# Second attention of a two-layer gated block: the unread matrix product behind each step is kept in the first of eight rounds only

## The reference, cut to what matters

```
x = x + tanh(g_xattn[0]) * attention0(layernorm(x), ctx)
x = x + tanh(g_ffn[0])   * quantised_ffn(layernorm(x))
query = (layernorm(x) @ w_q.T + b_q)   # 8 x 100 x 256, 16 heads
key, value = ctx @ w_k.T + b_k, ctx @ w_v.T + b_v   # 8 x 361 x 256
attn = softmax(query @ key^T / 4)      # per head, 100 x 361
x = x + tanh(g_xattn[1]) * ((attn @ value) @ w_o.T + b_o)
x = x + tanh(g_ffn[1])   * top2_of_8_experts(layernorm(x))
```

## Time and profile before

| | |
|---|---|
| median of 3 runs | 711.89 us (711.44 to 716.47) |
| the profiled execution | 715.0 us, span 713.3 us |
| mean granted TensorE clock in it | 0.867 of full |
| PE / DVE / ACT / POOL busy over the span | 75% / 60% / 42% / 21% |
| unread products, L1628 | 142 recorded, 49.2 us of PE busy time |
| second attention, rounds 0 to 7 | 398.4 to 511.2 us of the span |

### The profile page before, as it was taken

How to read it: one execution, slowest core, us unless ns; L and a number is a source line. 1 busy time by engine, 2 the same in 40 slices (tenths; PEclk the granted TensorE clock), 3 DMA queues, 4 the chain that set the end, 5 groups by cost and what they waited for, 6 DMA issues and landing times. The chain is left out here.

```text
span 713.3 us, 16026 instructions
## 1 busy us (share of the span) xinstructions
PE 533.2 (75%) x5585; PEld 381.5 (53%) x5585; DVE 430.0 (60%) x898; ACT 298.3 (42%) x480; POOL 146.4 (21%) x184
## 2 busy tenths in 40 slices
PE   0372778889878988736448898998754299999994
PEld 0261345556555656523223465666534288888884
DVE  7724567566666775466752777876467674444441
ACT  1074224555555445403304476775534132332221
POOL 1200002111111111100036212012122213434322
PEclk9995758999999986868859699998965599999998
DMA  8030673444534630000073578995293002122110
GB/s 254 6 108 21 106 150 83 111 108 105 120 96 107 162 91 24 1 0 1 0 144 90 168 142 163 207 159 111 62 346 107 29 17 39 29 40 43 31 26 1
DMA packets 73249, 64.34 MB, mean 90 GB/s; under 512 B 33326, under 2 KB 65750, under 8 KB 73190
## 3 DMA queue, kind: packets, MB, share of 16 engines
q1 hardware_dynamic: 61816, 41.78, 26.3%
q0 software_dynamic: 8224, 21.06, 11.0%
q10 hardware_dynamic: 3152, 0.71, 0.5%
HBM read 48.59 MB, written 15.92 MB: 90 GB/s over the span
## 5 line engine op out<-in xcount | busy, mean ns | idle before, releaser
L458 PEld LDWEIGHTS PS<-QS,KS 112*120 112x120 f16 (+2 forms) x896 | 81.9, 143 | 36.1 <-ACT PT L521 14.5
L458 PE MATMUL PS<-QS,KS 112*120 112x100 f16 (+2 forms) x896 | 92.5, 229 | 11.3 <-ACT PT L521 9.8
L569 DVE CUSTOM_DVE_ANT_0 PS<-PS,maskv 100x461 f32<-100x461 f32 x128 | 80.5, 646 | 14.4 <-PE PS L427 13.1
L572 DVE TENSOR_REDUCE mx<-PS 100x1 f32<-100x361 f32 x128 | 63.6, 529 | 36.2 <-PE PS L430 35.1
L521 ACT ACTIVATE PT<-PS,ctxb 120x400 f32<-120x400 f32 (+1 forms) x96 | 56.8, 593 | 51.9 <-PE PS L458 50.8
L521 ACT ACTIVATE PT<-PS 120x400 f32<-120x400 f32 (+1 forms) x128 | 63.1, 502 | 35.8 <-PE PS L458 33.3
L1969 PE MATMUL PS<-aT,WE 128*128 128x128 f16 x960 | 75.0, 221 | 0.3 <-issue 0.2
L1969 PEld LDWEIGHTS PS<-aT,WE 128*128 x960 | 66.2, 98 | 7.8 <-issue 1.4
L427 PE MATMUL PS<-KS,QS 65*100 65x461 f16 x128 | 51.4, 406 | 15.4 <-DVE mx L569 14.9
L779 POOL TENSOR_SCALAR_AFFINE_SELECT PT<-PT 100x400 f32<-100x400 f32 x32 | 17.6, 551 | 193.0 <-ACT PT L521 193.0
L1984 PE MATMUL PS<-WE,hidden_high 128*128 x320 | 55.6, 272 | 1.4 <-DVE hidden_low L2145 1.4
(11 more groups left out here) (301 smaller groups left out, 1072.5 us busy)
## 6 DMA issues: line engine op xcount, KB each, us to landing
share<-in_L_ffn_w_dram POOLq DMA_DIRECT2D x13, 1024.0 KB, 7.0
k_scratch<-share SPq DMA_DIRECT2D x32, 180.5 KB, 2.7
KS<-k_scratch SPq DMA_DIRECT2D x32, 180.5 KB, 3.7
KS<-k_scratch SPq DMA_DIRECT2D x64, 90.2 KB, 5.8
QS<-q_scratch SPq DMA_DIRECT2D x64, 50.0 KB, 2.5
v_scratch<-xn SPq DMA_DIRECT2D x8, 385.7 KB
values_staged<-v_scratch SPq DMA_DIRECT2D x8, 385.7 KB
WE<-in_L_ffn_w_dram POOLq DMA_DIRECT2D x2, 1024.0 KB, 8.6
```

The lines of the kernel that those rows point to most:

```text
L458: last = nc.tensor.matmul(bank[0:kn, i * T:(i + 1) * T], KS[p][:, h, k0:k0 + kn], QS[p][:, h, :], start=True, stop=True)
L569: nc.vector.tensor_tensor_reduce(rows, rows, maskv[:, :], 1.0, -BIG, ALU.add, ALU.max, mx[p][:, h:h + 1]).then_inc(s_smf, 1)
L572: nc.vector.tensor_reduce(mx[p][:, h:h + 1], sm_bank[h % 2][0:T, 0:TC], X, ALU.max).then_inc(s_smf, 1)
```

## The change

The unread product behind a step is issued only in round 0. In rounds 1 to 7 TensorE goes from the transposed scores of the step straight to what follows. That takes 84 of the 96 products inside the rounds away. The 46 in front of the rounds stay. No wait, no semaphore count and no other instruction is touched.

```diff
                         pe_ST(pe, j, o, t, 1, STN, 2 * B)
-                        unread()
+                        if first:
+                            unread()
                         if not first:
                             if t == PVL1:
```

## The result

| | before | after |
|---|---|---|
| median (lowest to highest) | 714.13 us (711.44 to 716.47) | 731.77 us (727.48 to 735.16) |
| executions | 4 | 4 |
| the profiled execution | 715.0 us, span 713.3 | 734.6 us, span 732.9 |
| mean granted TensorE clock in it | 0.867 | 0.793 |
| rounds 1 to 7 at a granted clock of 1.00 | all but some 7 us | 4 us |

The change makes the kernel slower by 17.6 us. The ratio is 1.0245 (1.0162 to 1.0328). The forecast was 716, with a range up to 720.5; it was worked out on a median before of 711.89 us, of the three executions known then.

A forecast was written before the change was run, and what follows sets the result against it. TensorE seemed the bound, with VectorE and DMA close behind. Changes of -0.2, +1.95, +1.95 and -0.9 us (transfer-limited savings, clock losses) gave +2.8; between 714.7 and 717.8 it took 716 us, range 708 to 720.5.

The forecast's parts named there:

- The upper bound of the gain: Rounds 1 to 7: removing 84 unread products of 0.22 us each frees at most 18.5 us of TensorE's work.
- VectorE's floor: Full-clock round with no transfer in the way: VectorE's 10.7 us plus 1.4 us of hand-overs, 12.1 us.
- The transfer's floor: Rounds 2, 4 and 6 start only when queries land behind the 1 MB load, 13.55 to 14.63 us after its issue.
- I expect the clock to fall at each of these three starts: Starts of rounds 2, 4 and 6: longer waits for queries and thinner work drop TensorE to half clock.
- I take 11 us: Half-clock stretch assumed in each of rounds 2, 4 and 6, costing 2.4 us apiece (bounds 1.5 and 3.3).
- The half-clock round, 15.4 us: A whole round without unread products at half clock, bound by TensorE: 15.4 us against 12.1 at full clock.
- An odd round that is still at half clock costs little more: Odd rounds: the next start waits for the transfer anyway, so half clock there adds little.
- C: Rival: the clock falls and stays down for whole rounds, each even round costing 3.3 us; +6.1, so 720 us; chance 0.21.
- D: Rival: queries issued earlier land earlier, so rounds 1 to 7 go by VectorE; 702 us; chance 0.05.

The follow-up runs named there:

- half_and_light: Kernel before with 256-column unread products in rounds 1 to 7 and, from the fourth on, expert-weight loads cut to a quarter (output not the reference's): ratio 0.9912.
- half_cols: Kernel before with unread products of rounds 1 to 7 cut from 512 to 256 columns: ratio 1.0017, median over all ten executions 721.5 us.
- ballast_even_rounds: Kernel before with the 12 unread products kept in rounds 0, 2, 4 and 6 and none in 1, 3, 5 and 7: ratio 1.0066.
- late_load: Kernel before with GpSimd issuing each load of expert weights six steps later, size unchanged: ratio 0.9999.
- change_light_load: The changed kernel with expert-weight loads cut to a quarter from the fourth on (output not the reference's): ratio to before 1.0244.
- ballast_odd_rounds: Kernel before with unread products kept in rounds 0, 1, 3, 5 and 7 and none in 2, 4 and 6: ratio 1.0013.
- quarter_cols: Kernel before with unread products of rounds 1 to 7 cut from 512 to 128 columns: ratio 1.0230.
- burst_8_at_start: The changed kernel plus 8 unread products behind the scores of step 0 in each of rounds 1 to 7: ratio to before 1.0008.
- alt_steps: Kernel before with 512-column unread products behind even steps only in rounds 1 to 7: ratio 0.9966, median over all ten executions 716.2 us.
- change_short_maxima: The changed kernel with row maxima of the second attention taken over the first 90 of 361 columns: ratio to before 1.0191.
- burst_at_start: The changed kernel plus 16 unread products at step 0 of each of rounds 1 to 7: ratio to before 1.0160.

## Why the prediction was wrong, point by point

*The upper bound of the gain, 84 times 0.22 us: right, and never reached.* The burst shows 3.45 us for 16 unread products, 0.216 each.

*VectorE's floor, 12.1 us: right in kind, 0.4 too low.* The same round at full clock took 12.47 and 12.50 us in the two kernels in which it kept the clock. The bounds, 10.7 and 13.3, held it, and it is not why the forecast failed. half_and_light fits: 1.0 us less work for TensorE made a round 0.37 us shorter.

*The transfer's floor: right in kind.* With less ballast the waits grew at the start of round 2 (1.38 to 1.61 in half_cols) and of round 4 (0.69 to 1.85), and with the small loads all waits were gone. The 2.5 us that were forecast were not seen in them; behind the thin round of ballast_even_rounds it is 1.67. My reasoning was by order as well (the queries queue behind the load); late_load shows that a later issue gains nothing. In the changed kernel, however, this floor of about 14 us is not reached, since its rounds take 17.2.

*"I expect the clock to fall at each of these three starts": this step failed.* It took the earlier trace rows as a rule about the length of one wait, 1.38 us against 1.73. The fall came at 419.2 in round 1, behind idle times of 0.41 us and less, before any of the three starts was reached, and in change_light_load in the same place with no transfer late. The table shows why a rule about one wait could not be right:

| kernel | what stood ahead | clock |
|---|---|---|
| before | wait of 1.38 us | held |
| before | wait of 1.73 us | fell |
| half_cols | waits of 1.61 and 2.02 us | held |
| half_cols | wait of 1.85 us | fell |
| ballast_even_rounds, ballast_odd_rounds | wait of 1.67 us, once in each | held, fell |
| quarter_cols, burst_8_at_start | waits of 1.64 and 1.03 us, wait of 1.88 us | fell |
| late_load, alt_steps, change_short_maxima | waits of 2.39, 3.16 and 3.70 us | fell |
| burst_at_start | 11.95 us of thin work behind 16 products, three times | held |
| the change, change_light_load | 5 us of thin work, idle times up to 0.41 us | fell |

In or behind most of the waits above 1.6 us the clock fell, so they count. But a wait is not needed: the work between counts as well, and how the two add up no run here shows. The page "TensorE: Matmul & The Clock Gate" of the Trainium skill (Part 1), with its rule that throttled is the default and activity lifts it, pointed the right way: the clock came back where unread products stood. The busy share in the profile did not tell when, though: the clock stayed at 0.50 while TensorE was recorded busy for 17.0 of 17.2 us in each round. I had used the page only for the direction of a cost that I then placed at the waits. The same page of the Trainium skill has a section, "A second HAM failure mode: psum-queue depth-cycling" (HAM is its name for what gates the clock), in which short idle times between groups of matmuls, not one long one, make the clock swing between its levels. The trace agrees as to the idle times (0.19 to 0.41 us) and differs as to the swing: here the clock went down once and stayed.

*"I take 11 us": failed.* I took the 6.82 us of the stretch in round 6 and stretched it. That stretch had unread products in it and this work has none: the clock stayed down for 122.9 us. With a quarter of the columns it came back after 27.3 us, in ballast_even_rounds after 17 us.

*The half-clock round, 15.4 us: mis-sized by 1.8, and this is the largest error in the price of a lost clock.* By term, 4.80 became 5.75 us for the scores, 4.88 became 5.83 for the score rows, 4.8 became 4.63 for the products with the values, and 0.9 became 1.02 for the turnings. The waits for maxima, which the sum left out, are 1.0 us of it (0.74 on the score rows, 0.26 on the scores); change_short_maxima shows them. The other 0.85 comes from taking one step of the earlier trace rows for all: the 0.40 and 0.305 us hold between scores and score rows, and not next to a product with the values or a turning.

*"An odd round that is still at half clock costs little more": failed by its size.* It would hold if a half-clock round of 15.4 us had to wait for a landing after 14 us anyway. But 17.2 is 3.2 us above that floor, and rounds 3 and 5, at 3.9 us each, paid more than any even one.

*The rivals.* C, the clock that falls and stays down, was the right one, and I had given it 0.21. Its price was wrong by three times, +6.1 where +19.5 came. That it let only the even rounds pay is the small part. With the prediction's own terms and all rounds at half clock it is six rounds of 15.4 and one of 11.5 against the 97.1 us of the earlier trace rows: +6.8, or 718.7 on the median of 711.9, still inside the range. What lacked is the size of the round, 6 x 1.83 = 11.0 us, and round 7, which grew by 2.9 us where C has 0.4. Less about 1 us for the full-clock start of round 1 this is +19.3. So a reader who had foreseen the fall, and kept 15.4, would have missed the time as well. For D the sum gives 701.4 and 700.6 us, not 702; nothing hangs on it.

## What to carry to other kernels

A product that nobody reads can be worth its time in a loop. Before taking such ballast out, work out the case in which the whole stretch runs at half clock, for every round of it, add the waits between the engines to the sum, take each distance from half-clock rows with the same neighbours, and let the range reach there. A clock loss seen behind one wait does not show that the wait alone caused it: look at how full the engine was before. And where two engines hand over to each other, what is taken from one of them is not all won: here 0.37 of 1.0 us, and 0.9 of 2.6.

## What the runs showed that was not expected

The clock's fall in the change repeats: it comes 4.1 to 4.2 us into round 1 in two executions of the change, in one of change_light_load and in one of ballast_even_rounds, whose round 1 is the same, and in the first three 122.9 us at 0.50 follow. The same thin work held 1.00 for 11.95 us when 3.45 us of unread products stood ahead of it. A thin round costs 17.24 / 12.47 = 1.38 times as much at half clock as at full, not twice. At full clock TensorE is busy for 10.84 of the 12.47 us, and part of what it loses in speed fills its idle time. And of the variants that keep the whole computation none was clearly faster than before; what was faster (0.9926) moved less data. What amount of work, and how placed, just keeps the clock stays open: half_cols, at 711 to 739 us, seems to stand near that edge.
